# A 512-step recurrence beside attention: the low part of the carry is made by GpSimd, not VectorE

## The reference, cut to what matters

```
h = four small attentions over the 512 positions (softmax(q k / scale) v)   # (8, 512, 128)
h = h + gated mix of two readouts of layernorm(h):
      reservoir:  new  = tanh(xt + prev @ W_res.T)        # one step for each of the 512 positions
                  prev = 0.95 * new + 0.05 * prev
      state space: h_t = A_bar_t * h_(t-1) + B_bar_t      # an elementwise recurrence
h = h + (a last layer that comes down to layernorm(h) of the 128 channels)
```

## Time and profile before

| | |
|---|---|
| median of 3 runs | 617.57 us (617.56 to 617.95) |
| the profiled execution | 617.05 us, span 615.2 us |
| busy share of the span | PE 93%, PEld 76%, DVE 86%, ACT 70%, POOL 31% |
| granted TensorE clock, mean | 0.991 of full speed |
| 384 steps beside attention | from 113.06 us to 452.76 us of the span |

### The profile page before, as it was taken

How to read it: one execution, slowest core, us unless ns; L and a number is a source line. 1 busy time by engine, 2 the same in 40 slices (tenths; PEclk the granted TensorE clock), 3 DMA queues, 4 the chain that set the end, 5 groups by cost and what they waited for, 6 DMA issues and landing times.

```text
span 615.2 us, 28453 instructions
## 1 busy us (share of the span) xinstructions
PE 574.3 (93%) x11143; PEld 466.8 (76%) x11143; DVE 528.1 (86%) x2340; ACT 427.7 (70%) x2244; POOL 191.2 (31%) x426
## 2 busy tenths in 40 slices
PE   6888888999999999999999999999999999999882
PEld 2554454788888888888888888888889988998871
DVE  6789997899878889988999999999767888899976
ACT  5576674577777777777777776777657677777764
POOL 1546364000000000010000000000000599898976
PEclk9999999999999999999999999999999999999978
DMA  6000000000000000000000000000020000000001
GB/s 218 2 2 2 2 1 2 3 3 3 4 3 4 3 4 4 4 4 3 4 4 4 4 3 3 4 4 4 3 72 3 3 20 16 19 20 16 20 16 30
DMA packets 8630, 8.32 MB, mean 14 GB/s; under 512 B 944, under 2 KB 7088, under 8 KB 8496
## 3 DMA queue, kind: packets, MB, share of 16 engines
q1 hardware_dynamic: 8208, 5.51, 3.1%
q10 hardware_dynamic: 288, 0.99, 0.5%
HBM read 3.35 MB, written 2.10 MB: 9 GB/s over the span
## 4 chain that ended last, share of the span: by engine, by line
PE 62%; POOL 24%; issue 9%; DVE 3%; DMA 1%; ACT 0%; POOLq 0%; SPq 0%; DVEq 0%
PE PS L1468 24%; PE PS L1515 16%; POOL prob_lo L442 4%; POOL r_dev L510 4%; PE PS L1486 4%; POOL ln_small L520 3%; PE PS L1417 2%; PE PS L1424 2%; PE PS L1418 2%; PE PS L1480 2%; PE PS L1475 2%; POOL k L496 2%; POOL k L533 2%; POOL ln_small L524 2%; POOL k L534 2%
## 5 line engine op out<-in xcount | busy, mean ns | idle before, releaser
L622 ACT ACTIVATE y<-PS 128x16 f16<-128x16 f32 x512 | 93.7, 183 | 134.1 <-PE PS L1480 124.1
L1515 PE MATMUL PS<-ballast,ident 128*128 128x245 f16 (+6 forms) x661 | 152.2, 301 | 0.0
L1027 DVE TENSOR_TENSOR y_lo<-ys,y 128x16 f16<-128x16 f32 x512 | 96.5, 188 | 47.0 <-ACT ys L623 37.8
L1468 PE MATMUL PS<-y_lo,res_hi 128*128 128x8 f16 x2048 | 128.8, 169 | 2.2 <-DVE y_lo L1027 1.1
L1468 PE MATMUL PS<-y,res_hi 128*128 128x8 f16 x2048 | 127.5, 168 | 0.1
L1468 PEld LDWEIGHTS PS<-y,res_hi 128*128 128x128 f16 x2048 | 96.4, 96 | 36.9 <-ACT y L622 18.5
L1468 PE MATMUL PS<-y,res_lo 128*128 128x8 f16 x2048 | 123.7, 166 | 0.0
L447 POOL TENSOR_TENSOR small<-small,minus_half 128x2 f32<-128x2 f32 x32 | 22.5, 704 | 305.6 <-DVE y_lo L1027 269.3
L623 ACT ACTIVATE ys<-PS 128x16 f32<-128x16 f32 x512 | 99.4, 194 | 0.0
L625 ACT ACTIVATE kp<-PS 128x16 f32<-128x16 f32 x512 | 98.4, 192 | 0.0
L1468 PEld LDWEIGHTS PS<-y_lo,res_hi 128*128 128x128 f16 x2048 | 85.4, 96 | 9.5 <-DVE y_lo L1027 3.1
(11 more groups left out here) (238 smaller groups left out, 1393.6 us busy)
## 6 DMA issues: line engine op xcount, KB each, us to landing
ys<-in_x SPq DMA_DIRECT2D x8, 256.0 KB, 7.7
out<-gate_all SPq DMA_DIRECT2D x24, 64.0 KB, 1.5
mats<-in_mats ACTq DMA_DIRECT2D x1, 709.0 KB, 5.0
h_last<-h_all SPq DMA_DIRECT2D x4, 128.0 KB, 3.2
gate_last<-gate_all SPq DMA_DIRECT2D x4, 128.0 KB, 2.9
out<-gate_last SPq DMA_DIRECT2D x16, 32.0 KB, 1.9
rows<-in_rows ACTq DMA_DIRECT2D x1, 257.5 KB, 7.6
wall<-in_wall SPq DMA_DIRECT2D x1, 256.0 KB, 4.8
```

Source lines behind the costliest of these rows:

```text
L622: a_.activation(y16[:, :].rearrange("p (m b) -> p m b", m=NH), pre, ACT.Tanh, scale=back).then_inc(y16_ready, 1)
L1027: v.tensor_tensor(y_lo[:, :], ys[:, :, bass.ds(i * STEPS + (1 + t), 1)].rearrange("p n o -> p (n o)"), y16[:, :], ALU.subtract).then_inc(l ...
L1468: t_.matmul(dst[:, m, :], wts[:, k, m * P:m * P + P], st[:, k * B:k * B + B], start=False, stop=False, skip_group_check=True)
L1515: t_.matmul(at[:, 0:size], ident16[:, :], ballast[:, 0:size], start=False, stop=True, skip_group_check=True)
```

## The change

Beside attention (the first 24 bodies, 384 steps) `kp_lo` is now made by GpSimd: the same subtraction on the same tiles, with the same wait for ScalarE's `kp`, is the first thing GpSimd does in each step, and it raises the same semaphore, `kp_lo_ready`. VectorE's step then holds `y_lo` alone, and no longer waits for `kp`. GpSimd's two operations a tile lose their wait on `lo_ready`; they stand behind the low part of steps 8 and 11 in GpSimd's order. From body 24 on, VectorE makes `kp_lo` as before.

```diff
             def work(p, j):
-                i = j + p // STEPS - AHEAD
                 if p == 24:
-                    pool.wait_ge(lo_ready, i * STEPS + p % STEPS + 2)
                     norm_root(j)
                 if p == 27:
-                    pool.wait_ge(lo_ready, i * STEPS + p % STEPS + 2)
                     gate_scale(j)
+
+            def carry_low(t, i):
+                pool.wait_ge(kp_ready, i * STEPS + (t + 1) + 1)
+                g.tensor_tensor(kp_lo[:, :].rearrange("p (m b) -> p m b", m=NH), kp[:, :].rearrange("p (m b) -> p m b", m=NH), kp_hi,
+                                ALU.subtract).then_inc(kp_lo_ready, 1)
...
             for i in range(FIRST_DECAY):
                 for p in range(STEPS):
+                    carry_low(p, i)
                     tiles_at(work, p, i + AHEAD)
...
-                dve.wait_ge(kp_ready, n + 1)
-                if i < FIRST_DECAY:
-                    v.tensor_tensor(kp_lo[:, :].rearrange("p (m b) -> p m b", m=NH), kp[:, :].rearrange("p (m b) -> p m b", m=NH), kp_hi,
-                                    ALU.subtract).then_inc(kp_lo_ready, 1)
-                else:
+                if i >= FIRST_DECAY:
+                    dve.wait_ge(kp_ready, n + 1)
                     v.scalar_tensor_tensor(kp_lo[:, :].rearrange("p (m b) -> p m b", m=NH), PRE[t % 2][:, r, :, t // 2, :], setup[:, 24:25],
-                                           kp_hi, ALU.mult, ALU.subtract
-                                           ).then_inc(kp_lo_ready, 1)
+                                           kp_hi, ALU.mult, ALU.subtract).then_inc(kp_lo_ready, 1)
```

## The result

The changed kernel takes 736.85 us (median of 4 runs, 733.49 to 740.55) against 617.76 us before: 1.192 times as long (95% interval 1.188 to 1.196). 688 was forecast, in a range of 631 to 703. The sign was right, and so was the blocking of GpSimd; the clock was not, and the loss was 119 us instead of 71. Medians here are over all runs of a kernel; ratios leave out a run that was more than 1.5% above the kernel's fastest.

A forecast was written before the change was run, and what follows sets the result against it. The prediction took a step's chain of waits from tanh to tanh as the bound; low parts 53.5, `difference` 6.9, other steps 10.2 and `norm_root` 0.2 made 70.8 us more, 688 us, range 631 to 703.

The forecast's parts named there:

- What bounds the kernel: Steps beside attention: a loop of latencies from tanh to tanh, 0.867 us; VectorE's `kp_lo` hangs beside it, 0.013 us early.
- GpSimd's start and length: GpSimd's `kp_lo` starts 0.412 us after tanh starts, takes 0.22, and reaches TensorE 0.048 later than the loop allows.
- The collision: VectorE's two-input operations start first and block GpSimd's `kp_lo`; beside a low part TensorE gets it 0.586 us later.
- `difference`: At t = 13 this two-input VectorE operation blocks GpSimd, 0.287 us more in each of 24 steps, 6.9 us together.
- Some 0.03 earlier: To go ahead of a two-input VectorE operation, GpSimd would have to start some 0.03 us before it.
- the 13 us of that rival: Rival, 6%: GpSimd is blocked to the end of VectorE's instruction, 0.11 us more in 117 steps, 701 us.
- The sum at the full clock: All added costs on the profiled execution of 617.05 us, without a fall of the clock: 70.8 us.
- low parts: 93 steps where VectorE's low part blocks GpSimd: 88 at 0.586 and 5 at 0.38 us, 53.5 us together.
- other steps: 213 steps without blocking that are not late: 0.048 us each for GpSimd's later `kp_lo`, 10.2 us.
- The 0.2 for `norm_root`: GpSimd's `norm_root` starts later in step 8 and delays `kp_lo` of step 9 by 0.01, 0.2 us for all 24.
- The clock falls too (20%): Rival, 20%: stalls in t = 10, 12, 14 and 0 bring TensorE's clock to 1.2 GHz, 11 us more, 699 us.
- The likeliest case: The prediction's own forecast, 40%: GpSimd is blocked by VectorE's two-input operations and the clock does not fall, 688 us.

The follow-up runs named there:

- e4: The changed kernel with one single-column VectorE memset ahead of each low part and each `difference` beside attention; 689.72 us, ratio 1.108.
- e5: The changed kernel with five single-column VectorE memsets ahead of each low part and each `difference` beside attention; 631.73 us, ratio 1.026.
- e3: The changed kernel with VectorE's low part beside attention replaced by a maximum over the same columns, with one SBUF input; 633.14 us, ratio 1.028.
- e1: The changed kernel with four more 240-column matmuls on zeros before TensorE's wait for `kp_lo` in steps after t = 0, 10, 12, 14; 682.74 us, ratio 1.106.
- e7: The kernel before the change, without any of the matmuls on zeros beside attention; 647.66 us, ratio 1.047.
- e6: The changed kernel without any of the matmuls on zeros beside attention; 705.44 us, ratio 1.135.

## Why the prediction was wrong, by its own steps

**What bounds the kernel:** right. The loop tanh, `ys`, `y_lo`, matmuls, `kp_lo` matmul was the limit, and the late steps t = 1 and t = 7 hid GpSimd's extra time (0.937 and 0.979).

**GpSimd's start and length:** right. It starts at T + 0.412 as worked out; 16 columns take 0.212, not 0.222. Its `kp_lo` reaches TensorE's load at T + 0.677, not T + 0.685, and an ordinary step grew by 0.034, not 0.048.

**The collision:** right, though it had 40% only. VectorE led by 5 to 14 ns in 115 pairs and won them all, and blocked steps took 1.436 against 1.45. The release fits what was read from the pair L1281 and L510: GpSimd's operation ended 0.07 after the low part did, which leaves 0.18 for its own work if it was let go 0.11 before the low part's end; the moment of release itself no record shows. `difference` was mis-sized by the same rule: 0.169 instead of 0.287. GpSimd's operation ended 0.025 before `difference` did, so by the same working this one lets go some 0.2 before its end, not 0.11. "Some 0.03 earlier" for GpSimd to win was wrong: e4 gives 6 ns, so the second pair of the earlier trace rows, where GpSimd was 0.02 ahead and still lost 0.04, has some other cause, which stays open. The rule of the Trainium skill (SBUF — State Buffer, Who interferes with whom) holds here in that the first to start goes first (e4, e5), and that an operation with one SBUF input, outside VectorE's two-port modes, does not block (e3); whether L830, the one that did, ran in such a mode, the trace does not show. "The whole instruction" the page says of the two-port modes; for two SBUF inputs it is 0.11 us too long here by that working, and too long in any case beside `difference`; the 13 us of that rival are not there.

**The sum at the full clock:** 70.8 us forecast, 64.4 measured by e1. The parts, from the medians of the steps: low parts 52 instead of 53.5, `difference` 4.1 instead of 6.9, other steps 7.2 instead of 10.2. The 0.2 for `norm_root` is not seen: GpSimd's `kp_lo` starts at T + 0.412 in t = 9 too.

**The step that failed** is "The clock falls too (20%)", with its price: 23 x 0.5 x (0.75 + 0.2) = 11 us. The likeliest case left the clock at 1.00, and the rival that had it fall was five times too small: 54 us (e1). Two things were wrong in the price. It charged the three steps between the stalls, and the clock did not come back behind them: it was low for 283 us of 459, once for 54.6 us on end. And so the steps that paid were others: t = 1 to 9, 121 of them at 1.2 GHz, pay 43 us, t = 15 another 5, the steps 11 and 13 between the stalls 2, the stalled ones 0.5; the rest is in steps during which the level changed. The price had 0.25 us for the padding of a step; those steps pay 0.29 to 0.45. In t = 2 and 3 the padding itself is longer by 0.19 (0.55 instead of 0.36), and the attention's matmuls make up the rest. In e7, where nothing is padded, the same clock costs an ordinary step 0.02.

The chance was too low as well. The prediction noted that PE would be busy for about 73% of the steps 14 to 0, beside 69% in the stretch before the clock fell once, and called that near, but gave the case 20%. Two windows of the changed kernel, the steps t = 14 to 0 of the seventh body and the steps t = 12 to 14 just ahead of the first fall (PE's busy time is the first one):

```profile
242.33:246.09 3.76, 2.94 (x71) 2.51 (x69) 1.89 (x6) 2.18 (x12) 1.70 (x3) 1.00 0.02 4
125.16:128.90 3.74, 2.90 (x64) 2.44 (x63) 2.37 (x9) 2.48 (x12) 1.88 (x4) 1.00 0.00 0
```

Both are 78% busy. Behind the second the clock fell, and behind the first it stayed at 2.4 GHz for 12 us more. So the busy share of the steps with stalls alone does not tell when the clock falls.

What stays open: what TensorE must do for the clock to fall or to come back. It stayed at 1.2 GHz through stretches in which PE's record has no gap:

```profile
337.30:353.60 16.30, 16.30 (x255) 13.38 (x255) 8.61 (x32) 6.86 (x44) 4.25 (x13) 0.50 0.01 3
```

## What to carry to other kernels

When a change adds several stalls in a row to TensorE in a kernel that is padded to hold its clock, reckon with the clock being lost and price the padding at the lower level in every step, not only where the stall is; or put the padding into the stall. Before moving a small operation of a loop to GpSimd, list VectorE's operations with two SBUF inputs that can be running when it starts, or start together with it; the wait can be about as long as the longest, and in a tie a few nanoseconds decide. An operation that hangs 0.013 us beside the critical loop has no room for an engine on which it starts 0.008 us later and takes 0.212 instead of 0.166.

## What the runs showed of the hardware that was not expected

- GpSimd beside VectorE: the order at the shared input is settled by the start to within some 6 ns (e4), unless another two-input operation is already running; the loser of a tie with a 512-column operation takes 0.77 instead of 0.21 us, the other way round the low part takes 0.75 instead of 0.68.
- A one-column memset between two VectorE operations moved the second by 0.016 us only, five by 0.127.
- In the changed kernel the granted clock stayed at 1.2 GHz for up to 54.6 us, with PE busy for 98% of that time, and in e6 for all of the window's 385 us, where nothing was padded and PE was busy for 86%.
- A kernel at 1.2 GHz for nearly all of the stretch beside attention, without padding (705 us), beat the same kernel with padding and a mean of 0.69 of the full clock beside attention (737 us).
